# A two-layer mixture-of-experts block on one core: router products of raw rows, and rows scattered once for both uses

## The reference

```
def ffn(x, w_router, w_gate, w_up, w_down):          # x is the layer norm of the state
    xt = x.reshape(T, H)
    probs = softmax(xt @ w_router); top1 = argmax(probs); gate = probs[top1]
    pos = (running count of tokens of the same expert) - 1
    accepted = pos < 640
    slot = where(accepted, top1 * 640 + pos, 32 * 640)
    buf[slot] = xt                                    # [32, 640, 256]
    y = (silu(buf @ w_gate) * (buf @ w_up)) @ w_down
    return xt + where(accepted, y[slot] * gate, 0)

x = x + 0.5 * ffn(ln(x), ...)
x = x + attention(ln(x), ...)
x = x + 0.5 * ffn(ln(x), ...)                         # same weights
```

## Time and profile before

| | us |
|---|---|
| median of 3 runs | 1674.33 |
| lowest and highest | 1673.36, 1679.4 |
| span of the profiled execution | 1587.6 |
| PE, ACT, DVE, POOL busy in the span | 1334.5, 1166.9, 1265.9, 770.7 |
| route / first experts / attention / second experts, ends at | 257, 663 + 36 of hand-over, 1181, 1587 |

### The profile page before, as it was taken

How to read it: one execution, slowest core, us unless ns; L and a number is a source line. 1 busy time by engine, 2 the same in 40 slices (tenths; PEclk the granted TensorE clock), 3 DMA queues, 4 the chain that set the end, 5 groups by cost and what they waited for, 6 DMA issues and landing times. The chain is left out here.

```text
span 1587.6 us, 31540 instructions
## 1 busy us (share of the span) xinstructions
PE 1334.5 (84%) x10174; PEld 1244.1 (78%) x10174; DVE 1265.9 (80%) x3493; ACT 1166.9 (74%) x2486; POOL 770.7 (49%) x917
## 2 busy tenths in 40 slices
PE   4546623999999999699999999997629999999997
PEld 3324413999999999599988898986619999999997
DVE  6576752999999999568899999998847877778775
ACT  6859923777777777479898898886647777777774
POOL 0067773344434444315557777876553434433443
PEclk8555555999999999899999999998859999999999
DMA  9999654667667667321222232211134444544541
GB/s 364 398 333 336 217 181 136 219 202 246 223 189 245 221 201 250 126 74 59 71 87 86 79 99 82 85 58 45 32 121 135 124 135 115 152 141 116 149 147 31
DMA packets 196882, 250.41 MB, mean 158 GB/s; under 512 B 24650, under 2 KB 182008, under 8 KB 192624
## 3 DMA queue, kind: packets, MB, share of 16 engines
q1 hardware_dynamic: 169072, 204.49, 40.5%
q0 software_dynamic: 27648, 43.91, 8.2%
HBM read 128.18 MB, written 152.47 MB: 177 GB/s over the span
## 5 line engine op out<-in xcount | busy, mean ns | idle before, releaser
L1041 PE MATMUL ps<-xs,ws 128*128 128x320 f32 x3072 | 465.5, 311 | 0.1
L1041 PEld LDWEIGHTS ps<-xs,ws 128*128 128x128 f32 x3072 | 455.5, 189 | 1.1 <-issue 1.1
L368 POOL DMA_INDIRECT slots<-xn,r x256 | 263.3, 1029 | 195.2 <-issue 76.4
L850 POOL DMA_INDIRECT x_rows<-ys,oidx x160 | 165.2, 1033 | 240.1 <-DVE ys L973 201.3
L850 POOL DMA_INDIRECT out<-ys,oidx x160 | 155.9, 975 | 246.8 <-DVE ys L962 184.2
L1041 PE MATMUL ps<-ws,hs 128*128 128x256 f32 x1920 | 262.0, 289 | 10.7 <-DVE ys L962 6.6
L1041 PEld LDWEIGHTS ps<-ws,hs 128*128 128x128 f32 x1920 | 239.0, 190 | 24.0 <-issue 22.3
L985 DVE TENSOR_TENSOR hf<-ps,sg 128x320 f32<-128x320 f32 x256 | 125.5, 490 | 85.7 <-ACT sg L904 84.6
L871 ACT CAST xs<-ps 128x512 fp32r<-128x512 f32 (+1 forms) x192 | 98.5, 513 | 129.7 <-PE ps L1034 129.7
L436 PE MATMUL ps<-cf,xn 128*128 128x128 f32 x512 | 110.7, 356 | 83.1 <-ACT xn L390 83.1
L925 DVE TENSOR_TENSOR ws<-wraw,ws 128x512 fp32r<-128x512 f32 x192 | 132.6, 692 | 58.2 <-ACT ws L864 55.5
(11 more groups left out here) (135 smaller groups left out, 2492.1 us busy)
## 6 DMA issues: line engine op xcount, KB each, us to landing
slots<-zero SPq DMA_DIRECT2D x32, 1300.0 KB, 9.3
xg<-slots SPq DMA_DIRECT2D x62, 650.0 KB
x_rows<-x SPq DMA_DIRECT2D x32, 516.0 KB, 9.3
x<-x_rows SPq DMA_DIRECT2D x32, 516.0 KB, 5.0
x<-in_x SPq DMA_DIRECT2D x32, 512.0 KB, 10.2
wraw<-in_w_gate SPq DMA_DIRECT2D x64, 256.0 KB
wraw<-in_w_up SPq DMA_DIRECT2D x64, 256.0 KB, 3.1
wraw<-in_w_down SPq DMA_DIRECT2D x64, 256.0 KB, 3.4
```

What stands on the lines that cost most here:

```text
L368: nc.gpsimd.indirect_dma_start(out=self.slots, out_offset=bass.IndirectOffsetOnAxis(ap=self.slot[:, t % self.xr, k:k + 1], axis=0), in_=se ...
L850: nc.gpsimd.indirect_dma_start(out=rows, out_offset=bass.IndirectOffsetOnAxis(ap=OIDX[:, e % YR, k:k + 1], axis=0), in_=YS[:, e % YR, k, : ...
L1041: ins = pe.matmul(dst, left(a, k), right(b, k), start=(n == 0), stop=(n == len(terms) - 1))
```

## The change

PE's router product is taken of raw rows: the transposes read x itself, and the router's weights have their column means subtracted on the chip, so that only the factor 1/sigma is left out. DVE puts it back by a product of the 16 x 32 shifted logits of each tile with 1/sigma (L479). The buffer `xn` and ACT's norm go. What is scattered is the row in x's own ring, by then the sum with half the norm, with its moments and four factor columns behind it (262 columns, HX to RW); A and B now give the norm from the sum, by a reciprocal and two steps that wait for one another. The ring is six batches deep. In layer 1 the slots and `x1_rows` are one tensor: a dropped row is scattered to its own place in it, and the 32 stores of route are gone. The fills write a large token number in place of the mask of empty slots (`dve_empty`, `out_index` and the mask go). `GAP` goes; the loads of quarters 4 to 11 stand behind every second fill.

The experts' `base` becomes `x_norm`, one expert earlier, into `XN`, and PE transposes that; `y_sum` adds in place. `XG` is five deep with three experts loaded ahead. In attention transposing and keeping are at 4 and 5 steps, the choice one to three steps earlier, and the last pairs' sums stand in the loop.

```diff
-R_ID, R_A, R_B, R_G = H, H + 1, H + 2, H + 3
-RW = H + 4
+F_ID, F_A, F_B, F_G = range(4)
+NF = 4
 HX = H + 2
+RW = HX + NF
 BIG = 3 << 20
-XR, RR = 3, 4
+XR, RR = 6, 4
+GR = 5
+AHEAD = 3
...
-        x1_rows = nc.dram_tensor("x1_rows", [T, HX], F32, kind="Internal").ap()
-        slots1 = nc.dram_tensor("slots1", [DROP, RW], F32, kind="Internal").ap()
+        slots1 = nc.dram_tensor("slots1_and_rows", [DROP + T, RW], F32, kind="Internal").ap()
+        x1_rows = slots1[DROP:DROP + T, 0:HX]
         slots2 = nc.dram_tensor("slots2", [DROP, RW], F32, kind="Internal").ap()
...
-            X = sb([P, XR, TB, HX], F32, name="x")
+            X = sb([P, XR, TB, RW], F32, name="x")
...
-                self.rb, self.nb, self.ve, self.mn = (s([P, RR, TB]) for _ in range(4))
+                self.rb, self.ve, self.hm = (s([P, RR, TB]) for _ in range(3))
                 self.s1, self.s2 = s([P, RR, TB]), s([P, RR, TB])
-                self.xn = s([P, rows_ring, TB, RW], F32, "xn")
...
             def pool_scatter(self, pool, c, u, bound):
                 t, lo, hi = CHOICES[c]
-                tiles = (lo + 2 * u, lo + 2 * u + 1)
                 pool.wait_ge(self.ready.sem, self.ready.at(c + 1))
+                pool.wait_ge(self.based.sem, self.based.at(NC * t + lo // CH + u + 1))
+                if not self.own:
+                    pool.wait_ge(self.noted.sem, self.noted.at(self.group_of[NC * t + lo // CH + u] + 1))
                 apart(pool)
-                for k in tiles:
+                for k in (lo + 2 * u, lo + 2 * u + 1):
+                    i = TB * t + k
                     nc.gpsimd.indirect_dma_start(
-                        out=self.slots, out_offset=bass.IndirectOffsetOnAxis(ap=self.slot[:, t % self.xr, k:k + 1], axis=0),
-                        in_=self.xn[:, t % self.xr, k, :], in_offset=None, bounds_check=bound, oob_is_err=False,
-                    ).then_inc(self.scattered[t % self.xr], 16)
+                        out=self.places, out_offset=bass.IndirectOffsetOnAxis(ap=self.slot[:, i:i + 1], axis=0),
+                        in_=self.rows_of(i), in_offset=None, bounds_check=bound, oob_is_err=False,
+                    ).then_inc(self.scattered[t], 16)
...
-            def act_norm(self, act, n):
...
             def pe_turn(self, pe, n):
-                pe.wait_ge(self.normed.sem, self.normed.at(n + 1))
                 pe.wait_ge(self.evac.sem, self.evac.at(n + 1 - len(self.bt)))
                 for j in range(CH):
                     for h in range(HC):
                         o = (h * CH + j) * P
                         ins = pe.transpose(ps[:, self.bt[n % len(self.bt)], o:o + P],
-                                           self.xn[:, n // NC % self.xr, CH * n % TB + j, h * P:(h + 1) * P], IDENT)
+                                           self.stream.tile(CH * n + j)[:, h * P:(h + 1) * P], IDENT)
...
-                                             ALU.mult).then_inc(self.chosen.sem, 1)
-                    dve.wait_ge(self.chosen.sem, self.chosen.at(c + 1))
+                                             ALU.mult).then_inc(links.sem, 1)
+                    dve.wait_ge(links.sem, links.next())
                     dve.reduce_max(rr, cand, AX).then_inc(links.sem, 1)
+                    dve.wait_ge(self.scaled.sem, self.scaled.at(self.group_of[NC * t + hi // CH - 1] + 1))
+                    apart(dve)
+                    dve.tensor_tensor(d, d, last(rb, E), ALU.mult).then_inc(self.chosen.sem, 1)
...
-                    dve.tensor_tensor(std, self.ve[:, t % RR, tiles], self.rb[:, t % RR, tiles], ALU.mult)
-                    dve.tensor_scalar(row[:, :, R_B], self.mn[:, t % RR, tiles], -1.0, None, ALU.mult)
-                    dve.tensor_copy(row[:, :, R_ID].bitcast(U32), TOK[:, TB * t + lo:TB * t + hi])
+                    dve.reciprocal(inv, s1).then_inc(links.sem, 1)
+                    own_row = TOK[:, TB * t + lo:TB * t + hi]
+                    if self.own:
+                        dve.tensor_scalar(row[:, :, F_ID].bitcast(U32), own_row, float(-DROP), None, ALU.add)
+                    else:
+                        dve.tensor_copy(row[:, :, F_ID].bitcast(U32), own_row)
+                    dve.wait_ge(links.sem, links.next())
+                    dve.tensor_tensor(row[:, :, F_A], inv, rb, ALU.mult).then_inc(links.sem, 1)
+                    dve.wait_ge(links.sem, links.next())
+                    dve.scalar_tensor_tensor(row[:, :, F_B], hm, 2.0, row[:, :, F_A], ALU.mult, ALU.mult)
...
-                    dve.tensor_scalar(row[:, :, R_A], std, 0.5, None, ALU.add)
...
-                    dve.scalar_tensor_tensor(t2, t1, float(DROP - 1 - BIG), acc, ALU.add, ALU.mult).then_inc(links.sem, 1)
-                    dve.scalar_tensor_tensor(row[:, :, R_G], gt, 0.5, acc, ALU.mult, ALU.mult)
+                    own_row = TOKF[:, TB * t + lo:TB * t + hi]
+                    dve.scalar_tensor_tensor(t2, t1, float(DROP - 1), own_row, ALU.add, ALU.subtract).then_inc(links.sem, 1)
+                    dve.scalar_tensor_tensor(row[:, :, F_G], gt, 0.5, acc, ALU.mult, ALU.mult)
                     dve.wait_ge(links.sem, links.next())
-                    dve.tensor_scalar(t1, t2, float(BIG), None, ALU.add).then_inc(links.sem, 1)
+                    dve.tensor_tensor(t1, t2, acc, ALU.mult).then_inc(links.sem, 1)
                     dve.wait_ge(links.sem, links.next())
-                    dve.tensor_copy(self.slot[:, t % self.xr, tiles], t1).then_inc(self.ready.sem, 1)
+                    dve.tensor_tensor(self.slot[:, TB * t + lo:TB * t + hi], t1, own_row, ALU.add).then_inc(self.ready.sem, 1)
...
+        def first_rows(sp, first):
+            sp.dma_start(XG[:, first % GR, 0:2], slots_of(first)[:, 0:2]).then_inc(xg_first, 16)
+            sp.dma_start(XG[:, first % GR, 2:ET], slots_of(first)[:, 2:ET]).then_inc(xg_in[first % GR], 16)
+            for e in range(first + 1, first + AHEAD):
+                sp.dma_start(XG[:, e % GR], slots_of(e)).then_inc(xg_in[e % GR], 16)
...
-                GAP = 10
-                def place(n):
-                    return n if n < 3 * NC else n + GAP
                 def put(S, lag):
-                    return [n for n in (S - lag, S - lag - GAP) if 0 <= n < NU and place(n) + lag == S]
+                    return [S - lag] if 0 <= S - lag < NU else []
...
-                    stream.load(sp, 4)
-                    stream.load(sp, 5)
+                    sp.wait_ge(blanked, 2)
                     for n in range(NFILL):
-                        fill(sp, 0, slots1, n)
-                        if n % 3 != 1 and 6 + n * 2 // 3 < 4 * XR:
-                            stream.load(sp, 6 + n * 2 // 3)
-                    for q in range(NQ4):
-                        sp.wait_ge(tail.noted.sem, tail.noted.at(tail.group_of[2 * q + 1] + 1))
-                        stream.store(sp, q, tail.based)
-                        if q >= 2 and q - 2 + 4 * XR < NQ4:
-                            stream.load(sp, q - 2 + 4 * XR)
+                        fill(sp, 0, n)
+                        if n % 2 == 1:
+                            stream.load(sp, 4 + n // 2)
+                    for q in range(4 + NFILL // 2, NQ4):
+                        if q >= 4 * XR and q % 4 == 0:
+                            sp.wait_ge(tail.scattered[q // 4 - XR], 16 * TB)
+                        stream.load(sp, q)
...
-                    stream.all_stored(sp)
                     tail.all_scattered(sp)
-                    first_rows(sp, slots1, 0)
+                    first_rows(sp, 0)
...
-                        for n in put(S, 0):
-                            tail.act_norm(act, n)
...
+                            for h in range(HC):
+                                dve.scalar_tensor_tensor(WR[:, h, :], ps[:, 4, 0:E], -1.0 / H, WR[:, h, :], ALU.mult,
+                                                         ALU.add).then_inc(s_prepd, 1)
...
+                    def x_norm(e, q):
+                        if e == first and q == 0:
                             act.wait_ge(xg_first, 16 * (turn + 1))
-                        act.wait_ge(xg_in[e % GR], 16 * (e // GR + 1))
-                        if e >= YR:
-                            act.wait_ge(y_out[e % YR], 16 * ET * (e // YR))
+                        elif q == (1 if e == first else 0):
+                            act.wait_ge(xg_in[e % GR], 16 * (e // GR + 1))
+                        if q == 0 and e >= 2:
+                            act.wait_ge(turned.sem, turned.at(NQ * (e - 1)))
                         apart(act)
-                        for k in range(ET):
-                            ins = act.activation(YS[:, e % YR, k, 0:H], XG[:, e % GR, k, 0:H], ACT.Identity,
-                                                 bias=XG[:, e % GR, k, R_B:R_B + 1], scale=XG[:, e % GR, k, R_A:R_A + 1])
-                        ins.then_inc(based.sem, 1)
+                        for k in range(2 * q, min(2 * q + 2, ET)):
```

(30 more changed lines are left out.)

338 lines of the change are left out of this document (146 added, 192 removed).

## The result

The changed kernel takes 1716.8 us (median of 4 runs, 1714.97 to 1718.27) against 1673.95 us of the kernel before beside it: a ratio of 1.0253, with a 95% interval of 1.0227 to 1.0278. It is slower by 42.9 us where 14.7 were forecast, and outside the range. Its profiled execution spans 1714.2 us and took 1715.99, 1.8 us more.

The account below looks back on a forecast made before the run. Limits by stage: DMA engines to 77 us, POOL's scatters in route, PE in experts, VectorE in attention. Route 8.4, starts 10, experts 0, attention 2, tail −5.7 sum to +14.7 on 1674.3: 1689.0 us; 8-in-10 range 1660 to 1701.

Parts of the forecast that it names:

- the 86.7 us: Distance between the shown profile's span (1587.6 us) and the median (1674.33 us), left as it was, differences summed on the median.
- the 9.8 us of gaps, which should go: Route: POOL's waits between scatters for slot numbers or evacuation would vanish, saving 9.8 us.
- Rival C: Route: POOL starves again after its late start, DVE having almost no margin; 9.8 us return, total 1698.8; chance 0.12.
- Route's start: Route: first scatter moves from 77.6 to 95.6 us, as quarter 11's load lands behind all 16 fills; +18.
- rival A: Route: load order does not hold the first scatter, POOL starts at 77.6; route −10.9, total 1669.7; chance 0.13.
- Two starts: Both expert stages' starts: ACT must first write normalised rows, 5.0 us each, +10 in all; bounds +3 to +14.
- Experts steady: Experts after their start: PE stays the limit at 12.13 us an expert, so 0.
- Attention steady: Attention up to the last x_new: DVE's added work +9, less 7 of waits, gives +2; bounds −12 to +9.
- I take 7 of these 16 back: Attention: of DVE's 8.6 + 7.7 us of waits for ACT's scan input and its own scan, 7 would go.
- rival B: Attention: ACT's relief shortens the steps to the low bound, −12 instead of +2; total 1675.0; chance 0.13.
- Tail: Attention after the last x_new: shorter lags make batch 7's slots ready sooner, −5.7; bounds −12 to 0.
- Rival D: Attention's tail: slots wait on counting and the scan as before, nothing saved; total 1694.7; chance 0.12.

Follow-up runs that it names:

- r5_split: Changed kernel with two experts' rows loaded ahead of a stage's opening barrier, the third behind it; 1613.21 us, ratio 1.0142, beside a kernel before of 1591.66.
- r2_early: Changed kernel with the x loads of quarters 4 to 13 standing among the fills; 1704.81 us, ratio 1.0209.
- r3: Changed kernel with rows of 1056 bytes instead of 1048; 1718.02 us, ratio 1.0289.
- r10: Changed kernel with an expert stage's first row loads issued behind the barrier instead of ahead of it; 1718.97 us, ratio 1.0301.
- r12: Changed kernel with the last six batches' scatters counted by two semaphores instead of one; 1724.41 us, ratio 1.0326.
- r13: Changed kernel with batch t's slot numbers in the columns of batch 7−t; 1721.0 us, ratio 1.0246.
- r8: Changed kernel with the product with 1/sigma on one tile of 16 only; 1612.42 us, ratio 1.0129, beside a kernel before of 1591.66.
- r7: Changed kernel with attention's lags and choice times as before the change; 1615.39 us, ratio 1.015, beside a kernel before of 1591.66.

## Why the prediction was wrong

**The base.** The step that failed first is the sentence that left the 86.7 us "as they are". They were taken for a constant outside the stages and were idle time inside them (27 us in route, 40 in the first experts, 15 in attention). So "the 9.8 us of gaps, which should go" was argued from an execution whose gaps were not those of the timed runs. On the quiet chip the stream shrinks by 13.6 us as said, even by more; on the timed chip gaps of 37.3 become 44.0, and the stream grows by 4.9. That is a difference of 18.5 us. Over the whole span the changed kernel loses 15.5 us more on the disturbed chip than the kernel before does (39.2 for 23.7 in the table, with r5_split standing for the changed kernel on the quiet one).

Rival C had the outcome and the place: POOL starves where it goes on to the next choice, six times. Its condition alone, DVE's margin of 0.8 us a batch, does not do it, since POOL runs without a gap where signals are in time. That so thin a margin lets every late signal through to POOL fits the six places, but no run changed the margin, so it is argued and not shown.

**Route's start**, +18 to 95.6: right. Measured +16.5 and +16.3, and r2_early takes back 12.7 and with it the time. The load behind 16 fills came not ahead of them but at 76.8 us, and rival A fell. The Trainium skill, page "DMA: Bandwidth & Descriptors", section "Queues, rings and completion order", has each engine take descriptors in ring order, and the trace agrees.

**Two starts**, 5.0 each: the term was mis-sized by half. ACT's norms and their hand-overs cost 4.3 (8.8 us from table load to product for 4.5), as worked out. What the sum did not hold is the barrier: POOL's DRAIN ends 5.2 us later in route and 5.7 to 7.1 later in attention. No row of the profile lists it, and neither the diff nor the order shows a reason. r3, r5, r10, r12 and r13 rule out the step from 1048 to 1056 bytes a row, the loads in flight, the number of semaphores and the place of the indices. What remains (that the source is now the ring of x itself is one candidate) was not tried, and the cause is open.

**Experts steady**, 0: right where signals are in time (−1.3 and +0.7). On the timed chip +4.1 and −2.8.

**Attention steady**, +2: too small, measured +4.7 and on the quiet chip +7.7, inside the bound of +9. The step that failed is "I take 7 of these 16 back". The stretch of r5 for which the earlier trace rows has the kernel before:

```profile
709.00:1163.00 454.00, 408.44 (x3510) 383.41 (x3513) 416.99 (x1057) 323.72 (x671) 282.67 (x406) 0.98 0.18 59
```

DVE is busy for 417.0 us where it was 407.0: +10.0, near the +9 of the sum. Its idle time falls from 39.0 to 37.0 us, so 2 came back and not 7. ACT's relief shows where it was expected (DVE's wait for ACT's scan input falls from 8.6 us to 2.9), but a wait for another of ACT's results grows from 0.5 to 2.4 and the waits for its own scan from 7.7 to 9.3; rival B fell. Of the +7.7, r8 puts 4.1 on the product and r7 3.2 on the shorter lags, which the sum had as a gain in the tail only. That DVE's product would be held by POOL's reads was also weighed; its mean is 698 ns for 702 of the nearest form in the earlier trace rows, and of its twelve large ones eleven took 0.68 us and one 0.87, so there is next to no such price.

**Tail**, −5.7: right, −6.5 and −6.6; r7 confirms it with 5.5. Rival D fell. One reading on the way was off. The scatter at 1157.37 did not wait for batch 7's slots (POOL sat idle for 0.30 us, as before any other); POOL was simply busy with earlier tiles. In r5 22 scatters stand behind the last x_new instead of 26, and the four, 5.1 us, are most of the gain.

On the timed chip the terms were: route +21.4 for +8.4, starts +18.5 for +10, attention +4.7 for +2, tail −6.5 for −5.7, the rest +1.1 for 0, in all +39.2 for +14.7; the profiled executions lie 3.7 us nearer together than the medians. On the quiet chip: route +2.7 for +8.4, starts +20.0 for +10, attention +7.7 for +2, tail −6.6 for −5.7, the rest −0.1 for 0, in all +23.7. So the sign would have held there (r5's ratio is 1.0142). The size would have come nearer, but partly by luck, since route's miss of −5.7 stands against +10.0 in the starts and +5.7 in attention. The gaps on a disturbed chip and the DRAIN made most of the 28.2 us by which the forecast was short.

Three figures of the prediction don't come out of its own terms: 18.0 − 9.8 is 8.2 and not 8.4, rival A's −10.9 for route would be −9.8, and half the distances to the terms' bounds, added, give 1666 to 1702 and not 1681 to 1697. None of them hides the miss.

## What to carry to other kernels

Set a profile's span beside the time of the same execution before using it (here they lie 1.8 us apart). If only a median of other executions is at hand and differs by much more, don't sum on it what was read in the faster execution. Before moving a load behind a block of fills, look whether the first indirect store hangs on it: here that cost 12.7 us. Count each barrier's slowest closing instruction as a term, and a lag's effect on the steady part as well as on the tail.

## What the runs showed of the hardware

The same kernel takes 1592 us on one chip and 1670 to 1675 on the others, with like busy times: on the latter, semaphore updates come late, from a tenth of a microsecond to 17 us. The kernel before loses 27.4 us so in route, 39.5 in the first experts, 15.2 in attention and 2.6 in the second experts. Why some chips do so is open.

POOL's DRAIN behind indirect stores ends a fixed time after the last of them, which hangs on the program: 9.23 us behind route in the changed kernel, on the quiet chip (r5_split) as on the disturbed ones, and 4.00 in both profiles of the kernel before. Behind attention it is 9.20 in all profiles of the changed kernel, but 2.06 and 3.50 in the two of the kernel before. In route it lasts 8 us longer than the last packet of the scatters, and POOL could already run another instruction. What in the program sets it is open. The Trainium skill, page "VectorE: DVE Perf Modes", section "The DRAIN you can't avoid", knows two things of that name: the flush after each VectorE operation, and the DRAINs of about 12 ns in the preamble and postamble, on all engines. The one at the end of this program's blocks is neither, and the page has no price for it.
